# V's bias in the last attention of a four-layer block: from ScalarE's read-out of the attention output to a product with the output weights on TensorE

## What is computed

```python
def moe_proj(W, b):                       # weights: [B, 4], two of the four not zero
    Wc = jnp.einsum('be,ecd->bcd', weights, W)
    bc = weights @ b
    return jnp.einsum('btc,bcd->btd', hidden_states, Wc) + bc[:, None, :]
q = moe_proj(Wq, bq); k = moe_proj(Wk, bk); v = moe_proj(Wv, bv)      # split into 16 heads
scores = jnp.einsum('bthd,bshd->bhts', q, k) / sqrt(8)
attn = jax.nn.softmax(scores, axis=-1)
out = jnp.einsum('bhts,bshd->bthd', attn, v).reshape(B, T, C)
return out @ Wo + bo
```

## Time and profile before

| what | before |
|---|---|
| runs (three) | 2307.3, 2315.14, 2315.15 us; median 2315.14 |
| the profiled execution | 2310.45 us, of which the span of the core's instructions is 2308.0 |
| busy over the span | PE 83%, DVE 71%, ACT 60%, POOL 47% |
| the stage L3f's pipeline | from about 2006 us to the end at 2308 us |
| busy from 2006 to 2308 (302.0 us) | PE 282.50, DVE 276.92, ACT 277.30, POOL 94.15 us |

### The profile page before, as it was taken

One profiled execution on the slowest core, in us unless ns is written; L12 is line 12 of the kernel. 1 busy time (PEld: TensorE's weight loads), 2 busy tenths in 40 slices (PEclk: granted clock), 3 DMA queues, 4 the chain that ended last, 5 costly groups with the idle time before them and its releaser, 6 DMA issues. The chain is left out here.

```text
span 2308.0 us, 87577 instructions
## 1 busy us (share of the span) xinstructions
PE 1917.2 (83%) x32111; PEld 1457.7 (63%) x32111; DVE 1627.8 (71%) x3515; ACT 1381.3 (60%) x3749; POOL 1076.2 (47%) x1268
## 2 busy tenths in 40 slices
PE   4999978979999799999899851989980593499998
PEld 3777745667777588887666531767760241377776
DVE  5888877857777698888566750766652365499998
ACT  4777775655555466555455520647760367299997
POOL 4666615843333155555677456007767214233332
PEclk9999978999999899999999975999995555599999
DMA  4211102000000120000111001014432230000000
GB/s 114 50 48 48 46 21 55 1 16 15 15 14 14 36 70 0 0 0 0 33 32 33 25 27 47 1 35 134 148 111 69 72 94 22 1 12 14 18 14 19
DMA packets 174353, 87.94 MB, mean 38 GB/s; under 512 B 70892, under 2 KB 168840, under 8 KB 174216
## 3 DMA queue, kind: packets, MB, share of 16 engines
q1 hardware_dynamic: 161576, 62.31, 10.0%
q0 software_dynamic: 7296, 21.38, 3.2%
q10 hardware_dynamic: 5344, 2.43, 0.4%
HBM read 66.13 MB, written 19.93 MB: 37 GB/s over the span
## 5 line engine op out<-in xcount | busy, mean ns | idle before, releaser
L1453 POOL TENSOR_TENSOR L1f_hl<-L1f_h,L1f_hh 128x512 fp32r<-128x512 f32 x128 | 167.2, 1307 | 126.1 <-DVE L1f_hh L1465 126.1
L1414 ACT ACTIVATE L1f_h<-L1f_H,L1f_w_b 128x512 f32<-128x512 f32 x192 | 132.0, 688 | 104.0 <-PE L1f_H L884 97.5
L383 POOL TENSOR_TENSOR L1a_wide<-L1a_flat,head_of_row 128x512 f32<-128x512 f32 x64 | 66.6, 1040 | 200.9 <-ACT L1a_flat L579 158.5
L383 POOL TENSOR_TENSOR L3f_wide<-L3f_flat,head_of_row 128x512 f32<-128x512 f32 x64 | 66.7, 1042 | 190.3 <-PE L3f_S L451 167.9
L1465 DVE CAST L1f_hh<-L1f_h 128x512 fp32r<-128x512 f32 x192 | 128.3, 675 | 31.3 <-ACT L1f_h L1414 30.2
L605 DVE TENSOR_REDUCE L1a_mx<-L1a_S 128x16 f32<-128x1024 f32 x64 | 78.4, 1225 | 81.1 <-PE L1a_S L451 81.1
L605 DVE TENSOR_REDUCE L0a_mx<-L0a_S 128x16 f32<-128x1024 f32 x64 | 78.4, 1225 | 40.1 <-PE L0a_S L451 40.1
L383 POOL TENSOR_TENSOR L0a_wide<-L0a_flat,head_of_row 128x512 f32<-128x512 f32 x64 | 66.5, 1039 | 86.1 <-ACT L0a_xhat L592 78.4
L1709 POOL TENSOR_TENSOR L2f_routed_hl<-L2f_routed_h,L2f_routed_hh 128x512 fp32r<-128x512 f32 x66 | 85.5, 1297 | 30.5 <-ACT L2f_routed_hh L1787 25.8
L1260 ACT ACTIVATE L0f_parts<-L0f_psA,L0f_w_logits 128x128 f32<-128x128 f32 x256 | 73.0, 368 | 37.5 <-PE L0f_psA L1319 37.5
L830 DVE COPY_PREDICATED L2a_weights<-L2a_mask_raw,L2a_S 128x1024 f32<-128x1024 int32 x64 | 86.0, 1343 | 3.7 <-PE L2a_S L746 3.7
(11 more groups left out here) (504 smaller groups left out, 6908.7 us busy)
## 6 DMA issues: line engine op xcount, KB each, us to landing
L0a_mask_raw<-mask SPq DMA_DIRECT2D x256, 32.0 KB
sorted_x<-L1f_zero SPq DMA_DIRECT2D x4, 1408.0 KB, 12.3
L2f_routed_xhat<-sorted_x SPq DMA_DIRECT2D x22, 256.0 KB, 3.8
sorted_y<-L2f_routed_y_out SPq DMA_DIRECT2D x22, 256.0 KB, 4.1
L0a_ctxT<-ctx_T SPq DMA_DIRECT2D x64, 64.0 KB
L1a_ctxT<-ctx_T SPq DMA_DIRECT2D x64, 64.0 KB
L1a_mask_raw<-mask SPq DMA_DIRECT2D x256, 0.1 KB
L2a_ctxT<-ctx_T SPq DMA_DIRECT2D x64, 64.0 KB
```

Of the source, the lines that this page charges most:

```text
L383: pool.tensor_tensor(wide[:, s], flat[:, s, :].rearrange("p (b n) -> p b n", b=B2).unsqueeze(2).broadcast_to([P, B2, 4, S]), c.head_of_row ...
L1414: act.activation(h[:, q % 3, :], psH[:, q % 2, :], ACT.Relu, bias=b1[:, q:q + 1]).then_inc(h_kept, 1)
L1453: pool.tensor_tensor(hl[:, q % 3, :], h[:, q % 3, :], hh[:, q % 3, :], ALU.subtract).then_inc(hl_pool, 1)
```

## The change

ScalarE's read-out becomes one plain copy of 128 columns (the branch that was there for calls without a bias). GpSimd spreads the two bias columns of the tile over 64 columns each, into a new ring `v_bias` (lag 4, after `wide` and in front of the output bias). TensorE multiplies this tile with the output weights into the PSUM columns of TY, in front of the projection of the attention output, which now adds to it.

```diff
@@ attention, with the buffers
         if moe:
+            v_bias, v_bias_made = sb("v_bias", [P, RING, B2, S]), sem("v_bias_made")
@@ GpSimd, after wide
+                if moe:
+                    for u, s in at(i, r, 4):
+                        wait(pool, y_done, u - 3)
+                        pool.tensor_copy(v_bias[:, s], moe["v_bias"][:, bass.ds(B2 * u, B2)].unsqueeze(2)
+                                         .broadcast_to([P, B2, S])).then_inc(v_bias_made, 1)
@@ TensorE, lag 7
                     wait(pe, oT_kept, u + 1)
                     wait(pe, xT_kept, u + 7, NT)
                     wait(pe, x_summed, u)
-                    pe.matmul(psTY[:, Y:Y + P], oT[:, s, :], w["o"][:, :], start=True, stop=True,
+                    if moe:
+                        wait(pe, v_bias_made, u + 1)
+                        pe.matmul(psTY[:, Y:Y + P], v_bias[:, s].rearrange("p b n -> p (b n)"), w["o"][:, :],
+                                  start=True, stop=False, skip_group_check=True)
+                    pe.matmul(psTY[:, Y:Y + P], oT[:, s, :], w["o"][:, :], start=not moe, stop=True,
                               skip_group_check=True).then_inc(y_done, 1)
@@ ScalarE, lag 7
-                    if moe:
-                        for b in range(B2):
-                            last = act.activation(oT[:, s, S * b:S * b + S], psO[:, ON + S * b:ON + S * b + S],
-                                                  ACT.Identity, bias=moe["v_bias"][:, bass.ds(B2 * u + b, 1)])
-                        last.then_inc(oT_kept, 1)
-                    elif v_bias_col is not None:
+                    if v_bias_col is not None:
                         act.activation(oT[:, s, :], psO[:, ON:ON + P], ACT.Identity, bias=v_bias_col
                                        ).then_inc(oT_kept, 1)
                     else:
                         act.activation(oT[:, s, :], psO[:, ON:ON + P], ACT.Copy).then_inc(oT_kept, 1)
```

## The result

Slower by 0.44%: 2321.59 us (median of seven runs, 2319.44 to 2323.09) against 2310.69 (seven runs of the kernel before, 2307.3 to 2315.15); the ratio is 1.0044, with a 95% interval of 1.0033 to 1.0055. That is 10.9 us more, where the prediction had 11.1. The profiled execution took 2321.59 us, its span 2319.5.

What follows compares the result with a forecast made beforehand. Two closed chains of hand-overs through TensorE were taken to bound the step; 0.22 us a step gave 9.5 in the loop, 0.9 before and 0.7 after, 11.1 on 2310.45, so 2322 us, range 2317 to 2328.

Steps and rivals of the forecast that it cites:

- The bound: Last stage's loop: two closed chains of hand-overs through TensorE set the step, 4.31 and 4.385 us, not busy time.
- ScalarE's term: ScalarE's read-out, one instruction fewer: gains 0.2 us a step, worth nothing to either closed chain.
- TensorE's term: Added product ahead of the second half of the transpositions: 0.22 us a step, not hidden; range 0.22 to 0.39.
- The step of 4.48: Loop step from 2135.78 to 2140.26: the one-step chain with a longer hand-over, since line 460 begins late.
- chain A: One-step chain: line 460 to the transpositions' second half, exp, `xhat`, line 460 again; 4.31 us, 4.59 at the loop's turn.
- GpSimd's term: Added 128x128 copy on GpSimd, idle two thirds of the turn: 0.26 to 0.6 us, costed at nothing.
- The sum: Whole stage: 0.73 us more a turn, 9.5 over thirteen turns, 0.9 before, 0.7 after; 11.1 in all, 2322.
- The signs: Loop trace: turn 18.5 to 18.6 us, projection loads 0.43, `xhat` releasing line 460 at 0.06, ScalarE idle 0.3 a step.
- ScalarE as the bound: Rival: ScalarE's 0.2 us a step counts, the kernel gets faster, 2305 to 2306, at most 2298; chance 0.1.
- only chain B would lengthen: Rival: only the two-step chain, TensorE to S then VectorE to its sum, lengthens; 0.11 a step, 2317; chance 0.17.
- GpSimd in VectorE's way: Rival: GpSimd's copy delays VectorE's `weights_both`, 0.27 us more a step, 16 us, 2327; chance 0.13 including a TensorE stall.
- a stall at the wait: Rival: TensorE stalls 0.17 us at its new wait, 0.35 a step, 21 us, 2331; chance 0.13 including GpSimd's copy delaying VectorE.

Runs made afterwards that it cites:

- two moves without any change of work: Changed kernel with `xhat` ahead of ScalarE's second exp, 2314.47 us; changed kernel with both output projection products behind the transpositions, 2311.56 us.
- the relief alone, the first run: Kernel before with ScalarE's pair of read-outs as one plain copy, V's bias left out, no product: 2308.73 us against 2309.09, ratio 1.0001.
- two cuts: Kernel before with `xhat` ahead of the second exp, 2309.7 us; with VectorE's sum into x ahead of the reciprocal, 2311.7; with both, 2306.61.

## Why the prediction was right

**The bound.** It held that no engine's busy share but the order of hand-overs names the bound. Shown: ScalarE, the busiest, gave up 0.24 a step and the loop got no shorter, and two moves without any change of work took 7 and 10 us out of the changed kernel's total, 5.7 and 7.0 out of its stage.

**ScalarE's term.** Taken as 0.2 a step and worth nothing in the chains. It is 0.24, and worth nothing in the loop. The exp follows TensorE by 0.03 or 0.04 with or without it. In the emptying pipeline, where the prediction set 0.25 less against 0.22 more, the relief alone gave 0.9 us and the product alone cost 1.0; together they are 0.1.

**TensorE's term.** Taken as 0.22. The loads of the output projection grew from 0.21 to 0.44, so the product itself took what the earlier trace rows showed. But the distance from the transposition's load to the end of the second half went from 3.24 to 3.50 in plain steps (2150.06 to 2153.56), 0.26. The 0.03 to 0.04 on top was not in the term; it is one reason why a turn became 0.81 longer in place of 0.73. The run without the wait shows that the wait is 0.01 of it; 0.02 lies ahead of Q and K, and why is left open. The step of 4.48, which the prediction took for chain A with a longer hand-over, is 4.72 now, with the load again 0.22 behind `xhat`; that reading held.

**GpSimd's term.** Costed at nothing with 0.26 to 0.6 as bounds: 0.29, in idle time. Its additions end at 2151.85, VectorE's `weights_both` starts at 2152.57; the two never met, and `weights_both` kept its 611 ns (610 before). The Trainium skill, "SBUF — State Buffer", section "Who interferes with whom", says that a VectorE instruction with two inputs from SBUF contends with a GpSimd instruction that reads SBUF; since the two never met, this was not put to the test.

**The sum.** The loop was sized at 9.5, and it gave 10.3. The written-out steps in front and behind were sized at 0.9 and 0.7, and they gave 0.5 and 0.1. So those two were too large by 1.0 in all and the loop too small by 0.8. That they nearly cancel, and that the total came within 0.2 us, is luck; the size of 0.2 a step is not. The 2322 also rests on the choice of base: the prediction added to the profiled execution's 2310.45 and not to the median of three, 2315.14, and seven executions then gave 2310.69.

**Telling it from no change.** The prediction held that under 0.5% can't be told from no change. The interval reaches 0.11% to either side, so the 0.44% is told clearly.

**The signs.** TensorE's first load of the projection to line 402's is 0.44 (0.43 foretold), `xhat` stands 0.05 ahead of the load (0.06), and VectorE waits before its maximum. ScalarE's idle time before its exp is 0.22 and not 0.3. That the view would name the sum no longer as releaser did not come true, and it was no fair sign, as said above.

**The rivals.** ScalarE as the bound fell with the first run. That only chain B would lengthen fell with the product made twice: 0.23 a step and not 0.11. GpSimd in VectorE's way, or a stall at the wait, fell with the run without either, whose loop is 0.6 us shorter and no more. The estimate of 0.16 for the two passes from the Trainium skill, "TensorE: Matmul & The Clock Gate", section "Back-to-back issue gap", would have made 0.5 a turn; the two loads stand 0.21 to 0.22 apart here, and the second product shows 0.23 a step.

## What to carry to other kernels

Where several engines are all over 95% busy, follow each hand-over in the timeline and its distance: one that is the same few hundredths in every step is a wait that binds, however busy the waiting engine looks. Add up the closed chain that they make, and price an edit by whether it lies in that chain; here 0.24 a step taken off the busiest engine was worth nothing in the loop, 0.22 added on another cost 0.20 a step, and the same again 0.23. Before work is added to an engine, see whether it can go behind the instruction that others wait for. With both products of the output projection behind the transpositions the stage is 3.9 us longer than before and not 10.9. That is one version, and part of it is the gain of moving the old product.

## What was not expected of the hardware

A step's length does not add up from its instructions to the last hundredth: the distance from the transposition's load to the output projection's grew by 0.035, and taking the wait away gave back only 0.01 a step. 0.02 of the rest lies ahead of Q and K, where no instruction was added; what makes it is left open. And two cuts that are worth 0.1 a turn each (17.74 and 17.73 against 17.83) are worth 0.32 together (17.51), since each left the other chain in force.
